# A graph kernel's attention phase: six weight buffers for five, the first two source tiles prepared before a projection ends, and four maxima moved into head 0

## The reference, cut to what matters

```
def gat_conv(x, src, dst, W, a_src, a_dst, bias, H, C, n):
    h = (x @ W).reshape(n, H, C)
    s_src = (h * a_src).sum(-1);  s_dst = (h * a_dst).sum(-1)
    e = leaky_relu(s_src[src] + s_dst[dst], 0.2)
    emax = segment_max(e, dst)
    ee = exp(e - emax[dst]);  denom = segment_sum(ee, dst)
    out = segment_sum((ee / denom[dst])[:, :, None] * h[src], dst)
    return out.reshape(n, H * C) + bias
...
x_norm = layer_norm(x, norm_g, norm_b)
out1 = gat_conv(x_norm, src, dst, W1, a_src1, a_dst1, b1, 4, 192, N)
out2 = gat_conv(out1, src, dst, W2, a_src2, a_dst2, b2, 2, 96, N)
L0 = concatenate([x, out2]) @ Wu + bu
x = layernorm(x + L0)
```

## Time and profile before

| quantity | us |
|---|---|
| median of 3 runs (lowest, highest) | 826.17 (824.02, 826.29) |
| profiled execution, its own time | 828.5 |
| its span | 826.5 |
| TensorE busy | 786.2 (95%) |
| VectorE busy | 584.6 (71%) |
| ScalarE busy | 301.5 (36%) |
| first matmul of head 0 | starts at 272.72 |
| end of the four heads' matmuls | about 408 |

### The profile page before, as it was taken

How to read it: one execution, slowest core, us unless ns; L and a number is a source line. 1 busy time by engine, 2 the same in 40 slices (tenths; PEclk the granted TensorE clock), 3 DMA queues, 4 the chain that set the end, 5 groups by cost and what they waited for, 6 DMA issues and landing times.

```text
span 826.5 us, 11896 instructions
## 1 busy us (share of the span) xinstructions
PE 786.2 (95%) x4286; PEld 661.3 (80%) x4286; DVE 584.6 (71%) x1133; ACT 301.5 (36%) x617; POOL 26.3 (3%) x36
## 2 busy tenths in 40 slices
PE   5899999999899899999999998899999999999997
PEld 4856666665665799999865788788898889999997
DVE  2778888785899999999589998866625532113444
ACT  5436666654532434343153554222211311111000
POOL 6100000000000500000000000000000000000000
PEclk9989999999989899999989999999999999999999
DMA  9400000000000501020000510000012000000111
GB/s 311 150 2 1 1 1 2 1 1 2 1 1 5 164 25 65 1 65 1 1 0 1 181 28 2 1 1 1 1 49 87 1 1 1 1 1 20 58 58 53
DMA packets 10540, 27.77 MB, mean 34 GB/s; under 512 B 665, under 2 KB 4075, under 8 KB 9968
## 3 DMA queue, kind: packets, MB, share of 16 engines
q1 hardware_dynamic: 10480, 26.97, 9.7%
HBM read 23.09 MB, written 3.88 MB: 33 GB/s over the span
## 4 chain that ended last, share of the span: by engine, by line
PE 80%; DVE 9%; issue 7%; ACT 2%; DMA 1%; SPq 1%; DVEq 0%
PE ps L1142 77%; DVE att L635 2%; DVE att L671 2%; PE ps L1231 1%; PE ps L1442 1%; DMA edges<-in_dst 1%; PE ps L1252 1%; DVE gw1lo L715 1%; PE ps L1287 0%; DVE scrap1b L517 0%; DVE stats L718 0%; DVE mx L517 0%; DVE out L658 0%; DVE scrap L517 0%; ACT att L978 0%
## 5 line engine op out<-in xcount | busy, mean ns | idle before, releaser
L1142 PE MATMUL ps<-g,att 128*128 128x193 f32 x800 | 134.5, 332 | 5.6 <-DVE att L635 5.6
L1142 PEld LDWEIGHTS ps<-g,att 128*128 128x128 f32 x800 | 133.5, 193 | 6.4 <-issue 6.2
L978 ACT ACTIVATE att<-att,ssrc 128x1250 f32<-128x1250 f32 x60 | 80.1, 1338 | 93.8 <-DVE att L671 93.5
L671 DVE SCALAR_TENSOR_TENSOR att<-uB,s 128x1250 f32<-128x1250 f32 x60 | 91.1, 1522 | 0.0
L1142 PE MATMUL ps<-wp,xT 128*128 128x388 f32 x240 | 89.6, 511 | 0.8 <-ACT xT L922 0.8
L635 DVE SCALAR_TENSOR_TENSOR att<-att,ct 128x1250 f32<-128x1250 f32 x60 | 88.0, 1467 | 1.2 <-ACT att L978 1.0
L1142 PE MATMUL ps<-yhi,ctr 128*128 128x384 f32 x200 | 67.7, 338 | 0.0
L1142 PEld LDWEIGHTS ps<-wp,xT 128*128 128x128 f32 x240 | 43.4, 193 | 25.5 <-issue 2.2
L732 DVE SCALAR_TENSOR_TENSOR ylo_a<-ps,dinv,yhi 128x384 fp32r<-128x384 f32 x32 | 18.9, 615 | 57.5 <-ACT yhi L850 57.4
L521 DVE TENSOR_TENSOR ohs_abc<-iota,sloT 128x256 bf16<-128x256 bf16 x120 | 34.8, 290 | 28.4 <-PE ps L1142 27.1
L1142 PE MATMUL ps<-ylo_a,ctr 128*128 128x384 f32 x160 | 54.1, 338 | 0.0
(11 more groups left out here) (256 smaller groups left out, 1448.6 us busy)
## 6 DMA issues: line engine op xcount, KB each, us to landing
uB<-u_dram SPq DMA_DIRECT2D x4, 1280.0 KB, 5.8
wux<-in_L_gnn_Wu SPq DMA_DIRECT2D x2, 2304.0 KB, 15.7
gw<-in_L_gnn_W SPq DMA_DIRECT2D x2, 2304.0 KB, 11.2
xs<-in_x SPq DMA_DIRECT2D x1, 3456.0 KB
out<-ybuf SPq DMA_DIRECT2D x9, 384.0 KB, 2.3
w<-in_L_gnn_W SPq DMA_DIRECT2D x2, 1152.0 KB, 7.2
w2x<-in_L_gnn_W SPq DMA_DIRECT2D x1, 576.0 KB, 7.8
wuo<-in_L_gnn_Wu SPq DMA_DIRECT2D x1, 576.0 KB
```

The source lines that it names most:

```text
L671: v.scalar_tensor_tensor(att[:, n % NA, 0:N], uB[:, hp % 2, 1, 0:N], s08[:, h, q:q + 1], uB[:, hp % 2, 0, 0:N], ALU.add, ALU.max).then_inc ...
L978: a.activation(at_, at_, ACT.Exp, bias=ssrc[:, h, q:q + 1]).then_inc(att_exp, 1)
L1142: return t.matmul(o, lhsT, rhs, start=start, stop=stop, **kw)
```

## The change

A sixth `att` buffer is added, in the memory of `ssB_c` (the row for the maxima of the second layer's first head, which is written after the four heads). Numbers are placed so that n = 0 and n = 1 take buffers 4 and 5, which don't overlap the weights `wux`. VectorE no longer waits for the ten copies before head 0, but only for the count matrix; it waits for the end of TensorE's `x_wu` before n = 2. The last two halves' copies on ScalarE stand behind exp(0) and exp(1), and TensorE waits for them at the first two banks of n = 0. Four of the ten maxima of head 3 are taken from before head 0 and put behind mult(3) to mult(6) of head 0. SyncE's program is unchanged.

```
-NA = 5
+NA = 6
+EARLY = 2
+LATE = 4
...
-        ssB_c = at("ssB_c", [P, NP], F32, R_BIG + NA * NP * 4)
-        uB = at("uB", [P, 2, 2, NP], F32, R_BIG + (NA + 1) * NP * 4)
+        ssB_c = at("ssB_c", [P, NP], F32, R_BIG + (NA - 1) * NP * 4)
+        uB = at("uB", [P, 2, 2, NP], F32, R_BIG + NA * NP * 4)
...
+        def att_place(n):
+
+            return (n + NA - EARLY) % NA
+
...  (every att[:, n % NA, ...] becomes att[:, att_place(n), ...])
-            for h in range(1, H1):
+            for h in range(1, H1 - 1):
                 maxima(h)
+            maxima(H1 - 1, 0, T - LATE)
...
-            v.wait_ge(x_added, 2 * X2)
+            v.wait_ge(ct_out, T + 2)
...
+                    if n == EARLY:
+                        v.wait_ge(dn_ps, 2 * T + 2 * X2)
+                        v.memset(att[:, 0:NA - EARLY, N:NP], 1.0)
                     v.scalar_tensor_tensor(att[:, att_place(n), 0:N], ...   (pre)
                     if q == 0 and nxt is not None:
                         give_u(nxt)
                     if q > 0:
                         mult(hp, q - 1)
+                    if hp == 0 and 3 < q < 4 + LATE:
+                        maxima(H1 - 1, T - LATE + q - 4, T - LATE + q - 3)
...
-            v.memset(att[:, :, N:NP], 1.0)
+            v.memset(att[:, NA - EARLY:NA, N:NP], 1.0)
...  (before the second layer's heads)
+            v.memset(att[:, NA - 1:NA, N:NP], 1.0)
...  (ScalarE, in head)
+                    if n < EARLY:
+                        x_half2(X2 - 1, n)
...  (ScalarE, before head 0)
-            for q in range(H1 - 1, X2 + 1):
-                if q < X2:
-                    x_transposed(q)
+            for q in range(H1 - 1, X2):
+                x_transposed(q)
                 x_out2(q - 1)
...  (TensorE, in head)
+                        if n == 0 and half == 0 and b < 2:
+                            t.wait_ge(x_added, 2 * (X2 - 1) + b + 1)
```

More of the change, by code:

```diff
@@ L605, in _, with maxima @@
             v.tensor_scalar(s08[:, :, :], ssrc[:, :, :], SLOPE - 1.0, None, ALU.mult)
-            def maxima(h):
+            def maxima(h, q0=0, q1=T):
                 v.wait_ge(bc_out, 3 * (h + 1))
-                for q in range(T):
+                for q in range(q0, q1):
                     v.wait_ge(cp_deg, 3 * (q + 1) + 4)
@@ L632, in mult @@
                 v.wait_ge(att_exp, n + 1)
-                a = att[:, n % NA, 0:N]
+                a = att[:, att_place(n), 0:N]
                 v.scalar_tensor_tensor(a, a, HUGE, ct[:, q, 0:N], ALU.min, ALU.mult).then_inc(att_ready, 1)
@@ L670, in head @@
                         v.wait_ge(att_used, n - NA + 1)
-                    v.scalar_tensor_tensor(att[:, n % NA, 0:N], uB[:, hp % 2, 1, 0:N], s08[:, h, q:q + 1], uB[:, hp % 2, 0, 0:N],
+                    if n == EARLY:
+                        v.wait_ge(dn_ps, 2 * T + 2 * X2)
+                        v.memset(att[:, 0:NA - EARLY, N:NP], 1.0)
+                    v.scalar_tensor_tensor(att[:, att_place(n), 0:N], uB[:, hp % 2, 1, 0:N], s08[:, h, q:q + 1], uB[:, hp % 2, 0, 0:N],
                                            ALU.add, ALU.max).then_inc(att_pre, 1)
@@ L976, in head @@
                     a.wait_ge(att_pre, n + 1)
-                    at_ = att[:, n % NA, 0:N]
+                    at_ = att[:, att_place(n), 0:N]
                     a.activation(at_, at_, ACT.Exp, bias=ssrc[:, h, q:q + 1]).then_inc(att_exp, 1)
@@ L1340, in head @@
                         rhs = g[:, q, h, :] if hp < H1 else h2x[:, q, h, :]
-                        last = mm(ps[:, acc_bank(hp, b), half * wid:(half + 1) * wid], att[:, n % NA, dt_ * P:(dt_ + 1) * P], rhs,
+                        last = mm(ps[:, acc_bank(hp, b), half * wid:(half + 1) * wid], att[:, att_place(n), dt_ * P:(dt_ + 1) * P], rhs,
                                   q == 0 and half == 0, q == T - 1, skip_group_check=True)
```

## The result

The changed kernel takes 832.19 us, the median of five runs (831.6 to 836.55), against 825.69 (824.02 to 826.29) for the kernel before beside it. The ratio is 1.0088, with a 95% interval from 1.0059 to 1.0117: 6.5 us slower, at least 4.9 and at most 9.7. The forecast was 834.7 in a range from 828.5 to 838.5, with a chance of 0.85 for slower. The profiled execution took 832.16, its span is 830.3.

What follows compares the result with a forecast made beforehand. TensorE, busy 95%, was taken as the bound, with VectorE nearly equal within heads. Start gains (-5.6, -3.2) are given back; 4.7 + 3.2 + 0.5 + 0.1 = +8.5 on a median of 826.17 gives 834.7, range 828.5 to 838.5.

Steps and rivals of the forecast that it cites:

- delay by the maxima: Head 0: four rounds take VectorE 4.18 against TensorE's 3.27, so mult(5), (6), (7) come about 0.6, 0.8, 0.9 late.
- The start: Before head 0: four maxima fewer save 5.5 us, tile 0 begins at 267.1 without a gap, and the whole 8.8 go.
- the edge: Between projection and head 0: 5.63 us gap plus 3.2 lost to low clock, together 8.8 us.
- The decisive step: SyncE's queue waits for 40 maxima until 289.6, not 265.8; head 1's row follows wux2, so pre(10) starts at 308.4.
- the prediction's bounds: Write to u_dram behind wux2: landing between 292.8, as if alone, and 303.4, behind all of wux2 plus 1.29.
- the write overtakes: Rival, SyncE's queue: the small write lands at 292.8, ahead of wux2; 829.7 to 832.9 us, chance 0.11.
- row in time: Rival, head 1: uB lands before about 297, VectorE goes on at 296.6; -2.3, 823.9 us, chance 0.08.
- GpSimd's adds: Before head 1: they start at 302.1 where VectorE is idle; costed at nothing, or 0.6 if lasting until 313.
- 3.2 (clock at the new restart): TensorE restarting at head 1: the idle time brings the lower clock again, 3.2 us, with 0 and 5 as ends.
- the 0.5 at the bank: Head 1's third bank: TensorE waits 1.0, of which some 0.5 overlaps the slow stretch, leaving 0.5.
- sum of 4.7 + 3.2 + 0.5: Delay around head 1: 4.7 for its late row, 3.2 for the clock, 0.5 for the bank; tile 12 +8.4.
- the sum: Whole kernel: start gains given back before head 1; row, clock, bank and 0.1 for the memset leave +8.5 us.

Runs made afterwards that it cites:

- experiment 4: Changed kernel with the loop-limit addition, but no maxima moved (six buffers and early tiles stay): 825.66 us, ratio 0.9997.
- experiment 5: As experiment 3, but only head 1's small write goes ahead; uB's load stays behind wux2: 832.46 us, ratio 1.0083.
- experiment 7: Experiment 3 with the four moved maxima reading 512 of 1250 columns: 819.42 us.
- experiment 2: The changed kernel plus experiment 1's register operations on loop limits: 834.36 us, ratio 1.0109.
- experiment 3: Experiment 2 with head 1's row written and loaded (uB) ahead of b2b, a2b and wux2 in SyncE's queue: 822.54 us, ratio 0.9963.
- experiment 6: Experiment 1 (five buffers, no early tiles) with only the four maxima moved into head 0: 838.93 us, ratio 1.0153.
- experiment 1: The kernel before, with window loop starts and ends held to their lower limit by a register operation: 826.16 us, ratio 1.0004.
- experiment 8: Experiment 3 with two maxima moved instead of four: 824.42 us, ratio 0.9979.

## Why the prediction was right

The forecast's mechanism holds, and its own steps can be set against the trace. Since the profiled execution of the changed kernel reached the projection's end 3.5 us earlier (263.58 for 267.09), positions are counted from there: P is that end. In the eleven profiled executions it lies between 263.6 and 269.7: 265.2 to 269.7 with five buffers, 263.6 to 269.2 with six. So the 3.5 is within the spread of executions.

| step | predicted | measured |
|---|---|---|
| wait at head 0's first tile | 0 | 0.69 |
| its first 40 instructions | 6.53 | 6.77 |
| delay by the maxima, start to start: tiles 5 and 6, tile 7 | 1.4, 0.9 | 0.9, 0.9 |
| `b2b` issued (last maximum) | P + 22.5 | P + 22.8 |
| `wux2` issued | P + 23.9 | P + 24.1 |
| from there to `uB`'s issue | 11.6 | 10.85 |
| `uB`'s issue to pre(10) | 5.8 | 5.9 |
| pre(10) | P + 41.3 | P + 40.8 |
| tile 10 on TensorE | P + 46.1 | P + 45.8 |
| tiles 10 and 11 | 10.2 | 9.9 |
| tile 12, against the kernel before | +8.4 | +7.6 |

**The start.** Right that the edge goes (0.9 of the 8.8 stay, 0.69 of them as a wait) and that it doesn't matter; experiment 4 shows that without the moved maxima only part of the gap goes (4.56 stay). The missed 0.69 is VectorE's: mult(0) was put 1.3 ahead of P and ended 0.4 behind it, since in this execution the projection's end was 3.5 us earlier, and VectorE's last maximum before head 0 only 1.8 (258.38, where 265.71 less four maxima is 260.19). In experiments 5 and 7 there is no gap.

```profile
262.51 1.46 DVE L642 SCALAR_TENSOR_TENSOR att<-att,ct 128x1250 f32<-128x1250 f32 x1
```

**The decisive step,** that SyncE's queue stands behind the count of the maxima and the row behind `wux2`, is shown by experiments 2 and 3: one edit in the order of that queue takes away 11.8 us. The write lands with `wux2`, not behind it with a time of its own. `wux2` is 11.8 on its way, from 287.70 to 299.5, and `uB`'s issue, which waits for the write, stood at 298.55, a little ahead of that. The write took 10.4 for 1.3; counted from `wux2`'s issue it is 10.85, nearer to the upper of the prediction's bounds (12.4) than to the lower (1.8). The rival "the write overtakes" is out, and so is "row in time", by VectorE's 10.99 of idle time.

The rule of the Trainium skill in "DMA: Bandwidth & Descriptors", section "Queues, rings and completion order", had two halves here. That descriptors are consumed in order in a ring agrees with the trace (10.4 us for a small write, and 15.1 from `wux2`'s issue until a second load has landed). That a later copy may complete earlier was seen in no more than that lead of about 1 us.

**GpSimd's adds.** Costed at nothing beside the idle engine, and they are: 2.50, inside VectorE's idle time.

**The mis-sized term** is "3.2 (clock at the new restart)" with the 0.5 at the bank. The prediction set tile 12 by TensorE (323.5) and put VectorE's mult(12) 0.4 ahead of it (323.1). In the trace VectorE is last: from pre(10) at 304.41 to tile 12 at 319.23 are 14.8 us, which is its work (predicted 14.7), and experiment 3 has the same 14.8 (294.99 to 309.80) without any idle time or low clock. So where the clock comes back soon, its loss (here 2.94 for eight instructions, 1.6 more than at the full rate) and the bank's wait (0.72 for 1.0) lie beside VectorE's collect, and are worth nothing. What the change costs is then one term, the row: pre(10) comes late, and everything follows at VectorE's pace. Only a clock that stays low adds something. Experiment 5 needed 324.44 - 308.11 = 16.3 for the same stretch, experiment 6 327.23 - 311.04 = 16.2, so some 1.5 more. The prediction's sum of 4.7 + 3.2 + 0.5 came out nearly right because VectorE's own chain ends at nearly the same point. That is a coincidence of these numbers: the term of 3.2 was no cost of its own. Measured are +7.6 for +8.4: 0.3 from tile 10, of which the write's landing is 0.75 with small delays against it, 0.4 behind it, and 0.1 where the prediction took the transposes' start (315.05) for tile 12's (315.16).

**The rest of the distance.** 834.7 was forecast, the median is 832.19. Of these 2.5 us, 0.9 is the sum (+8.5 for +7.6), 0.5 is the median of the kernel before (826.17 when forecast, 825.69 beside the changed kernel), and 1.1 lies between the traces' +7.6 and the medians' +6.5. The last isn't shown to be more than the runs' spread: the interval reaches 9.7, and experiments 1 and 2 differ by 8.2. The five runs stand in two groups, three of about 832 at a mean clock of 0.982, and 835.4 and 836.6 at 0.976 and 0.978.

## What to carry to other kernels

When work is moved later, list what counts it: a queue in program order hands the delay to everything that stands behind its wait, wanted or not. A small urgent transfer belongs ahead of a large one that nobody waits for, also where both are ready at the same time. A gap removed in front of a stage in which two engines are equally busy is kept only if the engine that gets the moved work isn't late at the stage's end: here some 8 us gone at the start became 3.6 in the best order with the same work.

## What the runs showed of the hardware that was not expected

**One restart pattern met different stretches of low clock.** The changed kernel and experiment 5 restart in the same way, eight instructions in 2.94, a bank's wait of 0.72, then 32. Those 32 took 5.90 in the one and 7.78 in the other. Experiment 5's timeline of TensorE and its windows:

```profile
313.06 2.94 PE L1164 MATMUL ps<-g,att 128*128 128x193 f32 x8 [8.49 <-DVE att L650]
316.72 7.78 PE L1164 MATMUL ps<-g,att 128*128 128x193 f32 x32 [0.72 <-DVE h2x L673]
...
324.44 15.85 PE L1164 MATMUL ps<-g,att 128*128 128x193 f32 x96
```

```profile
304.57:307.70 3.13, 0.00 (x0) 0.00 (x0) 0.00 (x0) 0.00 (x0) 2.51 (x6) 1.00 0.35 147
307.70:313.06 5.36, 0.00 (x1) 0.01 (x1) 4.88 (x8) 2.67 (x2) 0.00 (x0) 0.50 0.00 2
313.06:321.40 8.34, 7.62 (x23) 7.11 (x24) 8.16 (x18) 1.34 (x1) 0.00 (x0) 0.50 0.00 0
```

In both the lower level of 1.2 GHz (0.50) came some 3 us after TensorE had stopped (in the kernel before it came 4.8 after, at 271.9). It stayed until about 312.3 in the one, 2.9 us into the new work, and for 8.3 in the other, after 10.1 and 8.5 us of idle time. Experiments 2 and 6 restart in the same way, and their 32 took 5.90 after 9.89 us and 7.64 after 9.45. So a longer idle time did not bring a longer low clock; what sets its length isn't shown.

Whole runs differ with their clock too, also where TensorE doesn't restart at a head: the runs of experiment 7 at a mean clock of 0.988 took 817.5 to 819.6, those at 0.981 and 0.983 took 822.3 and 822.1. Of the first of these slower two there is a profile. It reached the projection's end at 268.39, 3.0 us later than experiment 3's, with granted clocks of 0.80 from 45 to 60 and 0.88 from 240 to 263 where experiment 3 has 0.90 and 0.95. That part of the kernel is the same in both.

**A short gap is enough.** Behind gaps of 3.41 (experiment 8) and 4.56 (experiment 4) the first 40 instructions took 8.45, where experiments 5 and 7 took 6.89 without a gap; the granted clock was 0.50 from 269.2 to 272.4 and from 271.9 to 275. Behind a gap of 0.69 they took 6.77.

**GpSimd's six adds** took 2.5 us in VectorE's idle time and in experiment 3, where they began at 303.17 beside the collect, which reads PSUM. They took 7.45 to 11.2 beside the pre and mult passes, as in the earlier trace rows, and these passes then took 1.71 for 1.45 to 1.51. Where they fall decides what they cost: 0.7 us of VectorE's time in experiment 8, nothing in experiment 3.
